# A routed block without its last stage: a token-major output to which the expert rows are added by DMA

## The chip, the cores and the metric

The kernel runs on one core of a Trainium2 chip. Its engines are PE (TensorE, matrix products into the PSUM banks), DVE (VectorE), ACT (ScalarE), POOL (GpSimd) and SP, which here only issues DMAs. Each runs its own instruction list in order and waits on semaphores. The metric is the device time of one execution, in microseconds (us).

## The reference

Eight sequences of 512 tokens, 128 channels. A modulated layer norm feeds a block of time mixing (a recurrence over tokens) and channel mixing; then a second modulated norm feeds a mixture of experts, whose result returns through a gate `gb`, one vector of 128 channels for each sequence:

```python
h = _layernorm(x) * (1 + cb) + sb
x = x + gb * _L0_ffn_ref(h, ...)
# in _L0_ffn_ref:
logits = x @ w_router.T                      # 16 experts, top 1
scores = sigmoid(logits) * mask
gate, up = split(einsum('eth,ehf->etf', scores.T[:, :, None] * x, gate_up_proj))
expert_out = einsum('etf,efh->eth', up * silu(gate), down_proj)
shared = (silu(x @ w_gate.T) * (x @ w_up.T)) @ w_down.T
out = shared + expert_out.sum(axis=0)
```

So each of the 4096 tokens has the residual x, plus gb times the shared expert, plus gb times the row of its one expert. All is float32.

## The kernel before

**Stage 1, attention and routing** (the loops over `NB + LAG`, batches of 512 tokens, four of them in flight). Activations are mostly channel-major: channels on the 128 partitions, tokens along the row. For batch b, DVE's `residual` makes the new residual `x3w`; ACT's `keep_x3` (L764) copies it to `x3_all`; PE's `t3` turns it to token-major in a bank for the norm's statistics. `route`, `chosen`, `rank` and `slots` find each token's expert and its slot in `sorted_rows`, a table in HBM sorted by expert, in which each expert has a room of its own. POOL's `scatter` (L400) writes 128 token rows a time by indirect DMA: 32 of them, four a batch. A row is 132 floats: the scored token and its number.

**Stage 2, shared expert** (`shared_up`, `shared_silu`, `shared_act`, `shared_down`, `shared_base`; batches in pairs after the first two). PE's order is up(0), down(0), a wait for the last slots, up(1), down(1), then up(b), up(b+1), down(b), down(b+1). `shared_base` (L636) adds gb times the result to `x3_all`, channel-major, where gb is one number for each partition. Meanwhile SP fills the rest of each expert's last block with pad rows (L315, 16 DMAs) and loads the first six row blocks into `xb` (L325).

**Stage 3, experts** (`NBLK` = 47 blocks of 128 sorted rows, enough for any split). Per block: SP loads the rows; PE turns them (`row_in`, L1030), multiplies by the expert's gate and up matrices (`gate_up`, 512 columns), turns the activation (`turn_act`, L1043) and multiplies by the down matrix (`down`). ACT copies the turned rows (L827), takes the silu (L831) and copies the result y (L838). DVE copies the token number (L680), makes the product (L681) and copies its transpose (L685). POOL scatters y to its token's row of `y_rows` in HBM (L423); rows with a number over the last token are dropped by the bounds check. PE's order in step s is `turn_act(s-3)`, `down(s-4)`, `row_in(s)`, `gate_up(s-1)`. PE enters the stage when the last `shared_base` is done. A float32 product of 128 or 512 columns shows as two matmul instructions in the trace, a transpose as one.

**Stage 4, the last.** When all scatters have landed, SP reads `y_rows` batch by batch (L333), PE turns it (L862, `turn`), DVE multiplies by gb and adds `x3_all` (L698), ACT's queue stores to the channel-major output (L851). The host transposes it.

The order of all this is written out by hand; no scheduler moves anything. Every helper product on PE has line L858.

Of the kernel before, what the change touches and what calls it, by code (L numbers as in the profile page):

```python
# [3 lines left out]
def program(nc, ins, out_t):  # L4
# [18 lines left out]
    ROW = C + 4  # L23
    ROOM = NB * T + P
    PADS = E * ROOM
    NOROW = NB * T
    LAG = 3
    DEPTH = 6
    ENDS = 4
# [4 lines left out]
    with ctx:  # L34
        def sb(name, shape, dt=F32):
            return ctx.enter_context(nc.sbuf_tensor(name, shape, dt))
# [25 lines left out]
        x3_all = sb("x3_all", [P, NB * T])  # L62
# [69 lines left out]

        at[0] = 0
        yt = [tiles(carve(T)) for _ in range(ENDS)]
        fin = [carve(T) for _ in range(ENDS)]
        pad_row = sb("pad_row", [P, ROW])

# [7 lines left out]

        sorted_rows = nc.dram_tensor("sorted_rows", [PADS + P, ROW], F32, kind="Internal").ap()
        y_rows = nc.dram_tensor("y_rows", [NB * T, C], F32, kind="Internal").ap()
# [19 lines left out]
        L_pads = Signal("L_pads", 1 + E, 16)  # L167
# [5 lines left out]
        K_rows = Signal("K_rows", NB)  # L173

# [51 lines left out]
        C_dn = Signal("C_dn", 1)  # L226
        C_base = Signal("C_base", 1)

# [5 lines left out]
        D_act = Signal("D_act", 2)  # L234
# [3 lines left out]
        D_y = Signal("D_y", 1)  # L238
        D_out = [Signal(f"D_out{q}", 1, 16) for q in range(DEPTH)]

        E_y = [Signal(f"E_y{q}", 1, 16) for q in range(ENDS)]
        E_t = Signal("E_t", 1)
        E_f = Signal("E_f", 1)
        E_out = [Signal(f"E_out{q}", 1, 16) for q in range(ENDS)]

# [19 lines left out]
        def _(sp):  # L265
# [12 lines left out]

            sp.dma_start(cT[:], ins["cT"]).then_inc(L_small.sem, 16)
# [39 lines left out]
            for j in range(NBLK):  # L319
                q, i = j % DEPTH, j // DEPTH  # L320
                at_row = nc.s_assert_within(sp.value_load(table[j:j + 1, 1:2]), 0, PADS,
                                            skip_runtime_bounds_check_because="the table makes it as min(row, PADS)")
# [6 lines left out]
            for b in range(NB):  # L329
                q, i = b % ENDS, b // ENDS  # L330
                if i:
                    sp.wait_ge(E_t.sem, E_t.after(b - ENDS))
                sp.dma_start(yt[q], y_rows[span(b, T), :].rearrange("(j p) c -> p j c", p=P)).then_inc(E_y[q].sem, 16)  # L333

        @block.gpsimd
        def _(pool):
# [11 lines left out]
            pool.memset(pad_row[:, 0:C], 0.0).then_inc(K, 1)  # L348
            pool.memset(pad_row[:, C:ROW].bitcast(I32), NOROW).then_inc(K, 1)
            pool.iota(rows[:, :, C:C + 1].bitcast(I32), pattern=[[P, NTT], [1, 1]], base=0, channel_multiplier=1).then_inc(K, 1)  # L350
            pool.memset(rows[:, :, C + 1:ROW], 0.0).then_inc(K, 1)
# [44 lines left out]
            def scatter(b):  # L396
                pool.wait_ge(A_rows.sem, A_rows.after(b))
                pool.wait_ge(B_slot.sem, B_slot.after(b))
# [20 lines left out]

            for j in range(NBLK):  # L420
                q = j % DEPTH
                pool.wait_ge(D_y.sem, D_y.after(j))
                pool.indirect_dma_start(y_rows, bass.IndirectOffsetOnAxis(number[q], 0), yb[q], None,  # L423
                                        bounds_check=NB * T - 1, oob_is_err=False).then_inc(D_out[q].sem, 16)

        @block.vector
        def _(dve):
# [205 lines left out]
            def shared_base(b):  # L633
                dve.wait_ge(C_dn.sem, C_dn.after(b))
                x3 = x3_all[:, span(b, T)]
                dve.scalar_tensor_tensor(x3, bank[shared_banks[b % 2][0]][:], modc[:, GB, b:b + 1], x3,  # L636
                                         ALU.mult, ALU.add).then_inc(C_base.sem, 1)
# [26 lines left out]
            dve.tensor_scalar(table[:, 1:2], passed[:, 1:2], float(PADS), None, ALU.min).then_inc(S, 1)  # L664
# [10 lines left out]
            def expert_act(j):  # L675
                q = j % DEPTH
                if j >= DEPTH:
                    dve.wait_ge(D_out[q].sem, D_out[q].after(j // DEPTH - 1))
# [8 lines left out]
            for s in range(NBLK + 2):  # L687
                if block_no(s - 2):
                    expert_aT(s - 2)
                if block_no(s - 1):  # L690
                    expert_act(s - 1)

            for b in range(NB):
                q, i = b % ENDS, b // ENDS
                dve.wait_ge(E_t.sem, E_t.after(b))
                if i:
                    dve.wait_ge(E_out[q].sem, E_out[q].after(i - 1))
                dve.scalar_tensor_tensor(fin[q], bank[q][:], modc[:, GB, b:b + 1], x3_all[:, span(b, T)],  # L698
                                         ALU.mult, ALU.add).then_inc(E_f.sem, 1)

        @block.scalar
        def _(act):
# [16 lines left out]
            modulation_rows(0)  # L719

# [55 lines left out]
            for s in range(NB + LAG):  # L776
                if batch(s):
                    norm_rows(A_n1, 0, s, flat(xtok), flat(ht))
                    if s == 0:
                        for n in range(1, NB // 2):  # L780
                            modulation_rows(n)
                        act.wait_ge(K_dve.sem, K_dve.after(0))
                if batch(s - 2):
                    norm_rows(A_n3, 2, s - 2, bank[bX2], n3t)
                    x2(s - 2)
# [47 lines left out]
            def expert_y(j):  # L833
                q = j % DEPTH
                act.wait_ge(D_dn.sem, D_dn.after(j))
                if j >= DEPTH:
                    act.wait_ge(D_out[q].sem, D_out[q].after(j // DEPTH - 1))
                act.copy(yb[q], bank[6 + j % 2][:, 0:C]).then_inc(D_y.sem, 1)  # L838

            for s in range(NBLK + 3):  # L840
# [4 lines left out]
                if block_no(s - 3):  # L845
                    expert_y(s - 3)

            for b in range(NB):
                q = b % ENDS
                act.wait_ge(E_f.sem, E_f.after(b))  # L850
                act.dma_start(out_t[:, span(b, T)], fin[q]).then_inc(E_out[q].sem, 16)  # L851
            for q in range(ENDS):
                act.wait_ge(E_out[q].sem, E_out[q].after(NB // ENDS - 1))

        @block.tensor
        def _(pe):
# [19 lines left out]
            pe.wait_ge(K_dve.sem, K_dve.after(0))  # L876
            pe.wait_ge(L_att.sem, L_att.after(0))
# [192 lines left out]
            for b in range(NB):  # L1070
                q, i = b % ENDS, b // ENDS
                pe.wait_ge(E_y[q].sem, E_y[q].after(i))
                if i:
                    pe.wait_ge(E_f.sem, E_f.after(b - ENDS))
                turn(bank[q], flat(yt[q])).then_inc(E_t.sem, 1)

# [33 lines left out]
```

## Time and profile before

| | |
|---|---|
| median of 3 runs | 395.59 us (393.89 to 396.46) |
| the profiled execution | 393.6 us, span 391.8 us |
| PE busy | 296.8 us (76%) |
| DVE, POOL, ACT busy | 244.0, 187.6, 179.3 us (62%, 48%, 46%) |
| chain that ended last | PE 30%, DVE 24%, POOL 21%, issue 13%, ACT 7%, DMA 3% |
| clock granted to PE, mean | 0.858 |

The span runs from the first to the last instruction. The chain is followed back from the last instruction, at each step to what released it; "issue" is time for which the profile shows no cause. The granted clock is a share of 2.4 GHz: 1.00 is that, 0.50 is 1.2 GHz. POOL's rows for indirect DMAs are the engine's own time on them, not the transfer's; "landing" is from issue until the semaphore has its count. The shares are averages over the four stages.

### The profile page before, as it was taken

Reading aid. Unit: us, or ns where it says so; the run is one execution under the profiler, and the core shown is the slowest. Engines: PE = TensorE matmul, PEld = TensorE weight load, DVE = VectorE, ACT = ScalarE, POOL = GpSimd, SP = SyncE. Lnnn points to the kernel's source line nnn. Section 1 sums busy time; section 2 is a strip of 40 time slices with the busy share of each in tenths; the row PEclk is TensorE's granted clock in tenths of the full one; section 3 lists DMA queues with packets and bytes.
Section 4 is the critical chain, followed back from the end, with each engine's and each line's share of the span. In section 5 each row is a group of like instructions: output and inputs, shape, how many; then the busy total and the mean of one; then the engine's idle time right before and its main releaser. Section 6 shows DMA issues by size and latency. Waiting matters only on the chain.

```text
span 391.8 us, 4364 instructions
## 1 busy us (share of the span) xinstructions
PE 296.8 (76%) x1140; PEld 171.7 (44%) x1140; DVE 244.0 (62%) x514; ACT 179.3 (46%) x436; POOL 187.6 (48%) x267
## 2 busy tenths in 40 slices
PE   4363667877668766877795586699989999999844
PEld 4223234334433534544453343334436666666532
DVE  5148596997989889789688342634335444444423
ACT  2541654947556666555372543222214444444300
POOL 4542726558678485656273534310003666666610
PEclk9956598996998888767889598699999999999955
DMA  6688000102011010010010100132002222222057
GB/s 182 175 241 321 28 0 4 51 0 60 22 47 35 0 54 29 0 41 21 0 49 8 41 14 14 50 97 49 0 1 56 75 75 82 71 77 71 4 155 274
DMA packets 28184, 25.22 MB, mean 64 GB/s; under 512 B 3682, under 2 KB 21734, under 8 KB 28160
## 3 DMA queue, kind: packets, MB, share of 16 engines
q1 hardware_dynamic: 24480, 18.57, 16.5%
q0 software_dynamic: 2528, 4.27, 3.4%
q10 hardware_dynamic: 1152, 2.10, 1.4%
q8 instruction: 10, 0.16, 0.2%
q14 instruction: 14, 0.11, 0.1%
HBM read 17.42 MB, written 8.49 MB: 66 GB/s over the span
## 4 chain that ended last, share of the span: by engine, by line
PE 30%; DVE 24%; POOL 21%; issue 13%; ACT 7%; DMA 3%; SPq 0%; POOLq 0%; DVEq 0%; ACTq 0%
PE bank L858 23%; POOL y_rows L423 11%; PE bank L862 5%; DVE work L524 4%; POOL sorted_rows L400 4%; POOL work L377 3%; ACT work L724 2%; DMA work<-y_rows 2%; DVE work L543 2%; DVE work L519 2%; DVE work L517 1%; DVE work L541 1%; PE bank L901 1%; POOL work L381 1%; DVE work L528 1%
## 5 line engine op out<-in xcount | busy, mean ns | idle before, releaser
L423 POOL DMA_INDIRECT y_rows<-work x47 | 46.2, 982 | 71.2 <-ACT work L838 41.9
L862 PE MATMUL bank<-ident,work 128*128 128x128 f32 x192 | 40.2, 362 | 52.9 <-ACT work L724 23.9
L862 PEld LDWEIGHTS bank<-ident,work 128*128 128x128 f32 x192 | 29.9, 185 | 75.0 <-ACT work L724 28.9
L858 PE MATMUL bank<-up_experts,work 128*128 x94 | 48.2, 595 | 0.0
L685 DVE COPY work<-bank 128x256 f32<-128x256 f32 x47 | 19.9, 424 | 37.7 <-PE bank L1043 37.7
L400 POOL DMA_INDIRECT sorted_rows<-rows,slot_i x32 | 36.5, 1140 | 14.4 <-issue 8.9
L858 PE MATMUL bank<-work,Fk 128*128 128x512 f32 x64 | 34.9, 652 | 5.7 <-DVE work L506 5.7
L724 ACT ACTIVATE work<-work 128x128 f32<-128x128 f32 x64 | 26.3, 487 | 23.5 <-POOL work L381 23.5
L375 POOL TENSOR_SCALAR work<-work 128x4 f32<-128x4 f32 x32 | 6.7, 210 | 59.5 <-DVE work L432 58.6
L377 POOL TENSOR_TENSOR work<-work,neghalf 128x4 f32<-128x4 f32 x32 | 33.2, 1038 | 2.7
L858 PE MATMUL bank<-work,Fv 128*128 128x512 f32 x64 | 33.3, 648 | 0.0
L724 ACT ACTIVATE work<-bank,work 128x128 f32<-128x128 f32 x64 | 24.1, 459 | 13.9 <-POOL work L381 13.8
L831 ACT ACTIVATE work<-bank 128x256 f32<-128x256 f32 x47 | 18.0, 383 | 25.4 <-PE bank L858 25.4
L858 PE MATMUL bank<-down_experts,work 128*128 x188 | 28.9, 276 | 0.1
L394 POOL TENSOR_TENSOR work<-work 128x512 f32<-128x512 f32 x16 | 16.8, 1068 | 23.5 <-ACT work L756 23.4
L524 DVE RECIPROCAL work<-work 128x512 f32<-128x512 f32 x8 | 26.8, 3346 | 0.0
L858 PEld LDWEIGHTS bank<-down_experts,work 128*128 128x128 f32 x188 | 24.7, 191 | 0.3 <-issue 0.3
L1043 PEld LDWEIGHTS bank<-ident,work 128*128 128x128 f32 x94 | 12.9, 139 | 25.6 <-DVE work L681 16.3
L819 ACT ACTIVATE work<-bank 128x512 f32<-128x512 f32 x16 | 9.4, 597 | 29.8 <-PE bank L858 28.7
L756 ACT ACTIVATE work<-bank 128x512 f32<-128x512 f32 x32 | 18.6, 601 | 5.8 <-PE bank L858 5.7
L631 DVE TENSOR_TENSOR work<-work,bank 128x512 f32<-128x512 f32 x16 | 10.9, 686 | 15.1 <-PE bank L858 14.4
L858 PEld LDWEIGHTS bank<-work,Fk 128*128 128x128 f32 x64 | 11.4, 210 | 19.3 <-DVE work L506 13.8
(161 smaller groups left out, 630.4 us busy)
## 6 DMA issues: line engine op xcount, KB each, us to landing
up_experts<-in_gate_up SPq DMA_DIRECT2D x2, 2048.0 KB, 11.7
work<-sorted_rows SPq DMA_DIRECT2D x47, 66.0 KB, 1.8
work<-in_x SPq DMA_DIRECT2D x8, 256.0 KB, 3.4
work<-in_xT SPq DMA_DIRECT2D x8, 256.0 KB, 3.1
work<-y_rows SPq DMA_DIRECT2D x8, 256.0 KB, 4.2
out_t<-work ACTq DMA_DIRECT2D x8, 256.0 KB, 3.9
sorted_rows<-pad_row SPq DMA_DIRECT2D x17, 66.0 KB, 1.6
y_rows<-work POOLq DMA_INDIRECT x47
```

The lines of the kernel that those rows point to most:

```text
L377: pool.tensor_tensor(rstd[n], rstd[n], neghalf[:], ALU.pow).then_inc(S.sem, 1)
L394: pool.tensor_tensor(relus[c], relus[c], relus[c], ALU.mult).then_inc(A_sqp.sem, 1)
L400: pool.indirect_dma_start(sorted_rows, bass.IndirectOffsetOnAxis(slot_i[:, n:n + 1], 0), rows[:, n, :], None).then_inc(B_out.sem, 16)
L423: pool.indirect_dma_start(y_rows, bass.IndirectOffsetOnAxis(number[q], 0), yb[q], None, bounds_check=NB * T - 1, oob_is_err=False).then_in ...
L524: dve.reciprocal(ek, ek).then_inc(S.sem, 1)
L685: dve.tensor_copy(aT[j % 2], bank[4 + j % 2][:, 0:F]).then_inc(D_aT.sem, 1)
L724: act.activation(dst[:, j * C:(j + 1) * C], src[:, j * C:(j + 1) * C], ACT.Identity, bias=shift[n][:, j:j + 1], scale=rstd[n][:, j:j + 1]) ...
L756: act.activation(relus[c], bank[(bFK, bFK2)[k % 2]][:], ACT.Relu).then_inc(A_relu.sem, 1)
L831: act.activation(sge[j % 2], bank[2 + j % 2][:, 0:F], ACT.Silu).then_inc(D_sg.sem, 1)
L858: return pe.matmul(out, w, x, start=start, stop=stop)
L862: last = pe.transpose(out[:, j * P:(j + 1) * P], src[:, j * P:(j + 1) * P], ident[:])
L1043: last = pe.transpose(bank[4 + j % 2][:, c * P:(c + 1) * P], acte[j % 2][:, c * P:(c + 1) * P], ident[:])
```

## The change

The output becomes token-major, with 31 blocks of spare rows behind the 4096 tokens, which the host cuts off. `x3` is kept token-major (`x3_rows`), copied by ACT from the bank in which `t3` turned it. The shared expert's down product is made with the tokens on the partitions, so gb runs along the row: POOL multiplies `Wd` by gb for each batch (`Wd_gb`, two buffers), and `shared_base` is a plain addition. SP stores each batch's base to the output (`base_out`), four before the pad copies and four behind them. Rows in `sorted_rows` grow from 132 to 260 floats: scored token, gb, number. gb comes there by four DMAs between on-chip buffers. Pad rows lie ready in HBM, each with a spare row's number of its own, and the 16 pad DMAs copy from there. In the expert stage DVE multiplies y by the row's gb and POOL adds the block to the output by an accumulating indirect DMA without bounds check, after all bases have landed. The last stage and `y_rows` are gone. In the diff below a header names the engine.

```diff
-    ROW = C + 4
+    ROW = 2 * C + 4
+    NUM = 2 * C
...
-    NOROW = NB * T
+    SPARE = NBLK - NTT
...
@@ SP (sync)
+            def base_out(b):
+                sp.wait_ge(C_base.sem, C_base.after(b))
+                sp.dma_start(tokens(out_t[0:NB * T].rearrange("(b t) c -> b t c", b=NB), b), tiles(x3_rows[:, b])).then_inc(C_out.sem, 16)
...
+            sp.wait_ge(K_gb.sem, K_gb.after(0))
+            for j in range(NT):
+                sp.dma_start(rows[:].rearrange("p (b j) r -> p b j r", j=NT)[:, :, j, C:2 * C], gb_rows[:]).then_inc(L_gb.sem, 16)
...
-            sp.dma_start(sorted_rows[PADS:PADS + P, :], pad_row[:]).then_inc(L_pads.sem, 16)
+            pads = sorted_rows[PADS:, :].rearrange("(k p) r -> p k r", p=P)
+            sp.dma_start(pads[:, :, 0:NUM], pad_row[:].rearrange("p (o r) -> p o r", o=1).broadcast_to([P, SPARE + E, NUM])).then_inc(L_pads.sem, 16)
+            sp.dma_start(pads[:, :, NUM:], pad_id[:]).then_inc(L_pads.sem, 16)
             for b in range(NB - LAG + 1, NB):
                 load_xT(b)
+            for b in range(NB // 2):
+                base_out(b)
+            sp.wait_ge(L_pads.sem, L_pads.after(0, 2))
             sp.wait_ge(B_table.sem, B_table.after(0, 1))
             for e in range(E):
...
-                sp.dma_start(sorted_rows[bass.ds(at_row, P), :], pad_row[:]).then_inc(L_pads.sem, 16)
+                sp.dma_start(sorted_rows[bass.ds(at_row, P), :], sorted_rows[PADS + (SPARE + e) * P:PADS + (SPARE + e + 1) * P, :]).then_inc(L_pads.sem, 16)
+            for b in range(NB // 2, NB):
+                base_out(b)
...
                 if i:
-                    sp.wait_ge(D_act.sem, D_act.after(j - DEPTH))
+                    sp.wait_ge(D_y.sem, D_y.after(j - DEPTH))
                 sp.dma_start(xb[q], sorted_rows[bass.ds(at_row, P), :]).then_inc(D_x[q].sem, 16)
...
-            for b in range(NB):
...
-                sp.dma_start(yt[q], y_rows[span(b, T), :].rearrange("(j p) c -> p j c", p=P)).then_inc(E_y[q].sem, 16)
@@ POOL (gpsimd), behind the loop that ends with scatter(7)
+            for b in range(NB):
+                if b >= 2:
+                    pool.wait_ge(C_dn.sem, C_dn.after(b - 2))
+                pool.tensor_tensor(Wd_gb[:, b % 2], Wd[:], gb_rows[:, b:b + 1, :].broadcast_to([P, FC, C]), ALU.mult).then_inc(C_scale.sem, 1)
+
+            pool.wait_ge(C_out.sem, C_out.after(NB - 1))
             for j in range(NBLK):
                 q = j % DEPTH
                 pool.wait_ge(D_y.sem, D_y.after(j))
-                pool.indirect_dma_start(y_rows, bass.IndirectOffsetOnAxis(number[q], 0), yb[q], None,
-                                        bounds_check=NB * T - 1, oob_is_err=False).then_inc(D_out[q].sem, 16)
+                pool.indirect_dma_start(out_t, bass.IndirectOffsetOnAxis(number[q], 0), yb[q], None,
+                                        compute_op=ALU.add).then_inc(D_out[q].sem, 16)
@@ DVE (vector)
-                dve.scalar_tensor_tensor(x3, bank[shared_banks[b % 2][0]][:], modc[:, GB, b:b + 1], x3,
-                                         ALU.mult, ALU.add).then_inc(C_base.sem, 1)
+                dve.tensor_tensor(x3_rows[:, b], bank[shared_banks[b % 2][0]][:], x3_rows[:, b], ALU.add).then_inc(C_base.sem, 1)
...
             def expert_act(j):
...
-                dve.tensor_copy(number[q], xb[q][:, C:C + 1].bitcast(I32)).then_inc(D_act.sem, 1)
...
+            def expert_y(j):
+                q = j % DEPTH
+                if j >= DEPTH:
+                    dve.wait_ge(D_out[q].sem, D_out[q].after(j // DEPTH - 1))
+                dve.tensor_copy(number[q], xb[q][:, NUM:NUM + 1].bitcast(I32)).then_inc(D_y.sem, 1)
+                dve.wait_ge(D_dn.sem, D_dn.after(j))
+                dve.tensor_tensor(yb[q], bank[6 + j % 2][:, 0:C], xb[q][:, C:2 * C], ALU.mult).then_inc(D_y.sem, 1)
+
+            for s in range(NBLK + 3):
                 if block_no(s - 2):
                     expert_aT(s - 2)
                 if block_no(s - 1):
                     expert_act(s - 1)
+                if block_no(s - 3):
+                    expert_y(s - 3)
-            for b in range(NB):
...
-                dve.scalar_tensor_tensor(fin[q], bank[q][:], modc[:, GB, b:b + 1], x3_all[:, span(b, T)],
-                                         ALU.mult, ALU.add).then_inc(E_f.sem, 1)
@@ ACT (scalar)
+            def gb_copy(n):
+                act.wait_ge(K_gbm.sem, n + 1)
+                act.copy(gb_rows[:, n * NT:(n + 1) * NT, :], tok(5 + n)).then_inc(K_gb.sem, 1)
...
             def keep_x3(b):
-                act.wait_ge(A_x3.sem, A_x3.after(b))
-                act.copy(x3_all[:, span(b, T)], x3w).then_inc(A_keep.sem, 1)
+                act.wait_ge(A_st[3].sem, A_st[3].after(b))
+                act.copy(x3_rows[:, b], bank[bT3][:]).then_inc(A_keep.sem, 1)
...
-            def expert_y(j):
...
-                act.copy(yb[q], bank[6 + j % 2][:, 0:C]).then_inc(D_y.sem, 1)
...
-                act.dma_start(out_t[:, span(b, T)], fin[q]).then_inc(E_out[q].sem, 16)
@@ PE (tensor)
+            for b in range(NB):
+                last = mm(bank[5 + b // NT][:, b % NT * C:(b % NT + 1) * C], modc[:, GB, b:b + 1].broadcast_to([P, P]), ident[:])
+                if b % NT == NT - 1:
+                    last.then_inc(K_gbm.sem, 1)
...
             def shared_down(b):
                 q = b % 2
                 pe.wait_ge(C_act.sem, C_act.after(b))
-                for c in range(FC):
-                    last = mm(bank[shared_banks[q][0]][:], Wd[:, c], sg[q][c], start=c == 0, stop=c == FC - 1)
+                pe.wait_ge(C_scale.sem, C_scale.after(b))
+                for j in range(NT):
+                    for c in range(FC):
+                        last = mm(bank[shared_banks[q][0]][:, j * C:(j + 1) * C], sg[q][c][:, j * P:(j + 1) * P], Wd_gb[:, q, c],
+                                  start=c == 0, stop=c == FC - 1)
                 last.then_inc(C_dn.sem, 1)
...
-            for b in range(NB):
...
-                turn(bank[q], flat(yt[q])).then_inc(E_t.sem, 1)
```

## Rows read from the trace of the kernel before

**Rows 1.** Chain of waits, last 26 us: start us, us, what

```profile
372.63 2.12 DMA y_rows<-work
...
374.89 0.39 SPq L333
...
388.54 0.75 DVE work L698
```

**Rows 2.** Stretches: busy us of each engine, granted clock, DMA share, GB/s

```profile
213.50:216.40 2.90, 0.01 (x1) 0.00 (x0) 2.69 (x6) 1.50 (x4) 0.89 (x3) 0.90 0.01 3
216.40:218.50 2.10, 1.97 (x8) 1.57 (x8) 0.76 (x2) 0.06 (x1) 0.06 (x1) 0.50 0.37 120
...
236.60:240.30 3.70, 3.70 (x8) 2.10 (x9) 0.76 (x2) 0.59 (x1) 1.47 (x3) 0.58 0.00 0
...
258.00:291.00 33.00, 32.88 (x76) 14.36 (x76) 12.82 (x19) 7.16 (x12) 0.00 (x0) 1.00 0.12 31
290.70:291.90 1.20, 0.18 (x1) 0.00 (x0) 0.75 (x1) 0.00 (x0) 0.00 (x0) 1.00 0.00 0
```

**Rows 3.** Timeline, start of the shared expert: start, us, engine, line, operation

```profile
250.19 3.53 PE L858 MATMUL bank<-work,Wd 128*128 128x512 f32 x4 [1.49 <-DVE work L631]
...
255.28 0.96 POOL L400 DMA_INDIRECT sorted_rows<-rows,slot_i  x1 [0.31 <-issue]
...
257.26 0.69 DVE L631 TENSOR_TENSOR work<-work,bank 128x512 f32<-128x512 f32 x1 [0.17 <-PE bank L858]
...
258.00 1.98 PE L858 MATMUL bank<-work,Wd 128*128 128x512 f32 x4 [0.85 <-DVE work L631]
```

**Rows 4.** Timeline, two of the pairs of shared_down

```profile
266.69 3.60 PE L858 MATMUL bank<-work,Wd 128*128 128x512 f32 x8
...
276.99 3.60 PE L858 MATMUL bank<-work,Wd 128*128 128x512 f32 x8
```

**Rows 5.** Timeline, end of the shared and start of the expert stage

```profile
290.92 0.75 DVE L636 SCALAR_TENSOR_TENSOR x_all<-bank,modc,x_all 128x512 f32<-128x512 f32 x1 [0.96 <-PE bank L858]
...
291.93 0.30 PE L1030 MATMUL bank<-ident,work 128*128 128x128 f32 x1 [1.05 <-DVE x_all L636]
```

**Rows 6.** Timeline, one step of the expert stage

```profile
357.45 1.02 PE L858 MATMUL bank<-up_experts,work 128*128 x2
...
358.73 0.42 DVE L685 COPY work<-bank 128x256 f32<-128x256 f32 x1 [0.82 <-PE bank L1043]
358.87 0.14 PEld L1030 LDWEIGHTS bank<-ident,work 128*128 128x128 f32 x1
...
359.09 1.02 PE L858 MATMUL bank<-up_experts,work 128*128 x2
359.13 0.41 DVE L681 TENSOR_TENSOR work<-work,bank 128x256 f32<-128x256 f32 x1
359.18 0.27 ACT L838 COPY work<-bank 128x128 f32<-128x128 f32 x1 [0.28 <-PE bank L858]
...
360.21 0.98 POOL L423 DMA_INDIRECT y_rows<-work  x1 [0.65 <-issue]
```

**Rows 7.** SP's row loads; page on them; last, xT's (256 KB)

```profile
266.32 4.42 SPq L325 DMA_DIRECT2D work<-sorted_rows  x6
...
work<-sorted_rows SPq DMA_DIRECT2D x47, 66.0 KB, 1.8
...
DMA to landing us min/median/max: 2.7/3.1/3.6
```

**Rows 8.** Timeline, end of the expert stage

```profile
371.12 0.27 ACT L838 COPY work<-bank 128x128 f32<-128x128 f32 x1 [0.55 <-PE bank L858]
...
372.63 0.98 POOL L423 DMA_INDIRECT y_rows<-work  x1 [0.30 <-issue]
```

**Rows 9.** Timeline, set-up

```profile
12.04 1.27 POOL L388 TENSOR_TENSOR work<-work,ca_rows 128x512 f32<-128x512 f32 x1 [2.65 <-ACT work L724]
...
17.65 1.65 ACT L724 ACTIVATE work<-work 128x128 f32<-128x128 f32 x4 [3.85 <-POOL work L381]
```

More of the change, by code:

```diff
@@ L61, in program @@
         h2_all = sb("h2_all", [P, NB * T])
-        x3_all = sb("x3_all", [P, NB * T])
+        x3_rows = sb("x3_rows", [P, NB, T])
+        gb_rows = sb("gb_rows", [P, NB, C])
+        Wd_gb = sb("Wd_gb", [P, 2, FC, C])
         rows = sb("rows", [P, NTT, ROW])
@@ L130, in program @@
         number = [carve(1).bitcast(I32) for _ in range(DEPTH)]
[L133 to L136, printed above, removed]
+        pad_row = sb("pad_row", [P, NUM])
+        pad_id = sb("pad_id", [P, SPARE + E, ROW - NUM])
         bank = [ctx.enter_context(nc.psum_tensor(f"bank{n}", [P, 512], F32)) for n in range(8)]
@@ L144, in tok @@
             return bank[n][:].rearrange("p (j c) -> p j c", c=C)
-        sorted_rows = nc.dram_tensor("sorted_rows", [PADS + P, ROW], F32, kind="Internal").ap()
-        y_rows = nc.dram_tensor("y_rows", [NB * T, C], F32, kind="Internal").ap()
+        sorted_rows = nc.dram_tensor("sorted_rows", [PADS + (SPARE + E) * P, ROW], F32, kind="Internal").ap()
         class Signal:
@@ L173, in program @@
         K_rows = Signal("K_rows", NB)
+        K_gbm = Signal("K_gbm", 2)
+        K_gb = Signal("K_gb", 2)
+        L_gb = Signal("L_gb", NT, 16)
         A_x = Signal("A_x", 1, 16)
@@ L237, in program @@
         D_dn = Signal("D_dn", 1)
-        D_y = Signal("D_y", 1)
+        D_y = Signal("D_y", 2)
         D_out = [Signal(f"D_out{q}", 1, 16) for q in range(DEPTH)]
[L241 to L244, printed above, removed]
         g1, b1, g2, b2, tm1, cm1, tdec, tfirst, tm2, cm2 = (vecs[:, n:n + 1] for n in range(10))
@@ L320, in _ @@
                 q, i = j % DEPTH, j // DEPTH
-                at_row = nc.s_assert_within(sp.value_load(table[j:j + 1, 1:2]), 0, PADS,
-                                            skip_runtime_bounds_check_because="the table makes it as min(row, PADS)")
+                at_row = nc.s_assert_within(sp.value_load(table[j:j + 1, 1:2]), 0, PADS + (SPARE - 1) * P,
+                                            skip_runtime_bounds_check_because="the table makes it as min(row, last)")
                 if i:
-                    sp.wait_ge(D_act.sem, D_act.after(j - DEPTH))
+                    sp.wait_ge(D_y.sem, D_y.after(j - DEPTH))
                 sp.dma_start(xb[q], sorted_rows[bass.ds(at_row, P), :]).then_inc(D_x[q].sem, 16)
@@ L347, in _ @@
                                pattern=[[1, P]], channel_multiplier=-1).then_inc(K, 1)
[L348 to L351, printed above, removed]
+            pool.memset(pad_row[:], 0.0).then_inc(K, 1)
+            pool.iota(pad_id[:].bitcast(I32), pattern=[[P, SPARE + E], [0, ROW - NUM]], base=NB * T, channel_multiplier=1).then_inc(K, 1)
+            pool.iota(rows[:, :, NUM:NUM + 1].bitcast(I32), pattern=[[P, NTT], [1, 1]], base=0, channel_multiplier=1).then_inc(K, 1)
+            pool.memset(rows[:, :, NUM + 1:ROW], 0.0).then_inc(K, 1)
             for t in (x1p, x2p):
@@ L397, in scatter @@
                 pool.wait_ge(A_rows.sem, A_rows.after(b))
+                if b == 0:
+                    pool.wait_ge(L_gb.sem, L_gb.after(0))
                 pool.wait_ge(B_slot.sem, B_slot.after(b))
@@ L663, in _ @@
             dve.wait_ge(S, 12)
-            dve.tensor_scalar(table[:, 1:2], passed[:, 1:2], float(PADS), None, ALU.min).then_inc(S, 1)
+            dve.tensor_scalar(table[:, 1:2], passed[:, 1:2], float(PADS + (SPARE - 1) * P), None, ALU.min).then_inc(S, 1)
             shared_base(0)
@@ L782, in _ @@
                         act.wait_ge(K_dve.sem, K_dve.after(0))
+                        gb_copy(0)
+                        gb_copy(1)
                 if batch(s - 2):
@@ L831, in expert_silu @@
                 act.activation(sge[j % 2], bank[2 + j % 2][:, 0:F], ACT.Silu).then_inc(D_sg.sem, 1)
-            def expert_y(j):
[L834 to L837, printed above, removed]
-                act.copy(yb[q], bank[6 + j % 2][:, 0:C]).then_inc(D_y.sem, 1)
-            for s in range(NBLK + 3):
+            for s in range(NBLK + 1):
                 if block_no(s):
@@ L1068, in _ @@
                     gate_up(s - 1, e_up)
[L1070 to L1074, printed above, removed]
-                turn(bank[q], flat(yt[q])).then_inc(E_t.sem, 1)
 def kernel(**inputs):
@@ L1105 @@
     ins = {n: nc.dram_tensor(f"in_{n}", a.shape, mybir.dt.float32, kind="ExternalInput").ap() for n, a in arrays.items()}
[L1106 removed]
+    out_t = nc.dram_tensor("out_t", (nb * nt + (2 * ne - 1) * 128, c), mybir.dt.float32, kind="ExternalOutput").ap()
     program(nc, ins, out_t)
     got = run_bass_kernel_spmd(nc, [{f"in_{n}": a for n, a in arrays.items()}], core_ids=[0])
[L1109 removed]
+    return np.ascontiguousarray(got.results[0]["out_t"][:nb * nt]).reshape(nb, nt, c)
```

27 lines of the change are left out of this document (5 added, 22 removed).

## The prediction

> **What bounds the kernel now.** I read the chain of waits first, at its end. The last expert scatter starts at 372.63 and has landed 2.12 us later, at 374.75; only then does SP issue the first read of y_rows (374.89), and the last vector instruction starts at 388.54 with a store behind it [rows 1]. So everything from 374.75 to the end of the 391.8 us span, 17.05 us, is the last stage, and nothing else runs beside it.
>
> Then the table of stretches, for TensorE (PE) and its clock. From 258 to 291, the shared expert, PE is busy 32.88 of 33.00 us at full clock, 2.4 GHz [rows 2]: what is added to PE there is added to the time. Two batches take 10.30 us (276.99 less 266.69) [rows 4]. The same table shows the clock's cost: PE did nothing for 2.90 us from 213.50 and the next matmuls ran at 0.50, 1.2 GHz; after another such gap 236.60 to 240.30 still averaged 0.58; a gap of 1.2 us from 290.70 kept 1.00 [rows 2].
>
> The expert stage repeats every 1.64 us (359.09 less 357.45), and PE sets it: two 512-column pieces of 0.43 us (1.72 us for four, by rows 4: 10.30 us over 24 pieces) and seven 128-column pieces in the remaining 0.78 us, so 0.11 us each [rows 4, 6]. GpSimd (POOL) needs 0.98 us and then waits 0.65 [rows 6]; at the end, with the last scatter already due, it idles only 0.30 us before it [rows 8]. POOL's own limit is therefore 0.98 + 0.30 = 1.28 us a block.
>
> **What the change removes.** The eight reads, 32 transposes, eight combines and eight stores, with SP's, PE's, DVE's and ACT's waits: 17.05 us [rows 1]. The new end is the landing of the last scatter.
>
> **The start of the shared expert.** This is the largest cost. shared_down(0) now waits for Wd_gb, which POOL makes behind its 32nd scatter. That one starts at 255.28 and takes 0.96 us [rows 3]; a multiply of 128x512 took 1.27 us [rows 9], so 128x256 about 0.64, and with 0.2 us of hand-over PE starts at about 257.1 in place of 250.19 [rows 3]: +6.9 us. Queued behind it on PE are shared_up(1) and all that follows; DVE and ACT wait with it. down(0) was cold already (four pieces in 3.53 us) [rows 3]; it becomes 16 pieces of 128 columns, which cold cost 0.246 us each (x8 in 1.97) [rows 2], 3.9 us: +0.5 with the later return of the clock (0 to 1.5).
>
> **The other seven shared_down.** 16 x 0.11 = 1.79 us in place of 4 x 0.43 = 1.72 on the bound engine: 7 x 0.08 = +0.6. The later Wd_gb each have a pair's 10.30 us to be made in [rows 4]. shared_base turns from 0.75 us into a plain addition (0.69, as row 257.26) [rows 3, 5]: -0.06, left out.
>
> **The start of the expert stage.** The first row block used to be on chip; PE's transpose started at 291.93, 0.26 us after the last base (290.92 + 0.75) [rows 5]. Now SP issues base_out(7) on that signal, reads the table, and only then loads. SP's reaction is 0.14 us [rows 1], an issue with its table read 0.82 us ((4.42 - 0.33) / 5) [rows 7], so the load starts about 1.0 us behind the base and lands 2.1 us later, and the 256 KB store ahead of it in SP's queue (2.5 to 3.1 us for such sizes, as xT) may hold it to about 3.3: 3.3 - 0.26 = +3.1 us (2.6 to 4). The 16 pad copies stand behind base_out(3), but 16 x 0.82 = 13 us fit before the last base. PE is then idle for over 4 us, longer than the gap that halved the clock [rows 2]; the 0.58 from 236.60 to 240.30 is 3.1 us at half speed, 1.6 us lost, of which the filling pipeline hides part: +1.3 (0 to 2).
>
> **The loop over the row buffers.** The buffer is freed later: before, DVE's product freed it; now the gated product of y, two steps later. Follow one round. gate_up starts at 357.45; its product runs 359.13 to 359.54, so 2.09 us on. In DVE's order the number copy and the y of two blocks earlier come next: 0.06 + 0.32 (a 128x128 product by the line through 0.41 for 256 and 0.69 for 512 columns is 0.27 us, and 0.05 of start) makes 2.47 us [rows 3, 6]. Then 0.14 for SP, the load, 0.09 to reach PE, and 0.22 from row_in's weight load (358.87) to gate_up (359.09) [rows 6]. This y is block j - 6, whose step stands three steps ahead of row_in(j), so the period is at least (2.92 + load) / 3. A load of 528-byte rows lands in 1.8 us [rows 7]: 1.57, hidden. Rows are now 1040 bytes. xT, 128 rows of 2048 bytes, takes 2.7 at best, 3.1 in the middle [rows 7]; interpolated, 2.1 to 2.25. I take 2.1, and with the accumulate's traffic beside it 2.15: 1.69 us a block, +0.05 over the 41 blocks that reuse a buffer = +2.0 us. Bounds: 0 (a load of 1.95 is hidden) and +8 (2.6, 1.84 us a block).
>
> The Trainium skill, DMA: Bandwidth & Descriptors, Anatomy of one DMA, fits a DMA as a constant plus bytes at 436 GB/s, for the GpSimd path. By it the 65.5 KB more would cost 0.15 us, the loop would stay hidden, and the sum would be 2.0 us lower. The xT row, 0.9 us more for 194 KB at its best, speaks for the dearer line here.
>
> **DVE and ACT in this loop.** DVE's idle 0.82 us a block before the copy of L685 takes in the 0.3 [rows 6]; ACT loses 0.27. No cost, while the period is over 1.3 us. POOL gets y 0.4 us later, once: at the end y's last piece comes 0.27 us behind PE either way, and three scatters in a row at 1.28 make +0.3.
>
> **The accumulating scatter.** No row shows one. Nearest are the plain scatters, 0.96 and 0.98 us on POOL and 2.12 us to landing [rows 1, 3, 8]. Lower bound: the same. Upper bound: twice the POOL time, since it handles two sources for each row. I take the same POOL time, by those rows, and +0.4 for the last landing (0 to 2). A price up to 1.38 us on POOL is hidden by the 1.69 us loop.
>
> **Small edits.** The 16 pieces for the gate on PE (1.8 to 3.9 us by the rates above) and two ACT copies fall in the 3.85 us in which ACT idled before row 17.65 [rows 9]: +0.3 (0 to 1). The x3 copy waits for statistics that the normalisation behind it waits for anyway: 0. Wider scatters have as many rows: 0. Four 0.5 MB gate copies (512-byte pieces) behind the expert weights, and 4 MB of pads in two DMAs on SP's queue, run where that queue is nearly idle; the next loads have several us: 0, and if SP is held past xT(6)'s issue, some us.
>
> **Sum.** -17.05 + 6.9 + 0.5 + 0.6 + 3.1 + 1.3 + 2.0 + 0.3 + 0.4 + 0.3 = -1.65. The profiled execution took 393.6 us, 2.0 under the median of 395.59; carried to the median, 394.
>
> **Rivals.**
> (A) The waits stay small: clock restarts hide in the pipeline, the load lands in under 1.95, the scatter is plain. -17.05 + 6.9 + 0.6 + 2.6 + 0.5 = -6.4, about 389. For it: three of my terms have 0 as a bound. Against it: the 6.9 and 2.6 are order in the code.
> (B) Slower: POOL becomes the bound of the expert stage through the accumulate. It decides from 1.38 us a scatter on (0.98 now). At one and a half times, 1.47 + 0.30 = 1.77 a block, 47 x 0.13 = +6.1 in place of +2.0: 398. At twice, 2.26, +29 in place of +2: 421. For it: POOL's time is per row, and rows get a second source. Against: 0.98 holds a fixed part, and bounds checking goes.
> The Trainium skill, Collectives: The Full Stack, Stop 4, shows an adding DMA as two reads and one write, and its GPSIMD Engine Reference, When to use GPSIMD, has one core write the read descriptors and another the write descriptors; by that the reading core's work doubles, the 421 end of this rival. No row here shows it.
> (C) The accumulate's extra read and write slow the loads beside it: a landing of 2.8 gives 1.91 us a block, +11: 403. Before, they shared the engines with plain scatters and stayed at 1.8 [rows 7], against it.
>
> **Chances.** Forecast 0.42, A 0.20, B 0.25 (a third of it at the far end), C 0.13. About 1%, 4 us, is what a measurement tells from no change. Faster by more: A, mostly, and a little of the forecast: 0.22. Within: 0.38. Slower: B, C and the forecast's upper part: 0.40. The likeliest case alone spans 390 to 398. The range takes in A nearly whole, C, and B at half more: 389 to 408.
>
> **What would show it.** PE idle from before 250.2 until about 257, with POOL's multiply ending it; row_in(0) some 3 us behind the last base, at clock 0.50; gate_up every 1.69 us and row_in waiting for DMA, not POOL; scatters of 0.98 us; the end 2.5 us behind the last scatter's start. Scatters over 1.38 us, or gate_up at 1.64 us with no clock loss, would make it wrong, upwards or downwards.

## The result: 3% slower

The changed kernel took 407.14 us (median of 4 runs, 406.25 to 408.11), the kernel before 395.22 beside it (4 runs, 393.89 to 396.46): ratio 1.030, 95% interval 1.026 to 1.035. The profiled execution took 406.78 us, its span is 404.5, against 393.6 and 391.8 before. Here and below a median is over all runs of a kernel and a ratio over its faster runs alone, because the times of one kernel fall into groups some 6 us apart; so a ratio need not be that of the two medians. The forecast was 394; what came is rival B and, on top, an end that no case had.

**Profile after.** From the page: POOL's busy time, and its busy tenths in 40 slices of 10.1 us, where the last stage is gone and POOL stands at 8 from slice 32 on:

```profile
PE 295.5 (73%) x1220; PEld 178.5 (44%) x1220; DVE 247.2 (61%) x553; ACT 172.1 (43%) x391; POOL 221.6 (55%) x275
...
POOL 5542636558557584873444523501101888888884
...
L438 POOL DMA_INDIRECT out_t<-work x47 | 73.5, 1564 | 36.3 <-DVE work L703 24.7
```

The line of the output scatter (duration min/median/max in ns, first and last start; then the landings) answers to the 0.98 us and 2.12 us of [rows 1, 8]:

```profile
L438 POOL DMA_INDIRECT out_t<-work x47: 1559/1562/1634, 311.5 to 397.5; - x47
...
DMA to landing us min/median/max: 3.2/3.4/4.4
```

1.56 us, and 0.30 of issue behind each: the chain of waits (start, us, what) goes from one scatter to the next and finds no other engine:

```profile
380.69 1.56 POOL out_t L438
382.26 0.30 issue
382.56 1.56 POOL out_t L438
```

Next the timeline at the start of the shared expert, which answers to [rows 3]. POOL's multiply follows the 32nd scatter, and PE, idle for 8.48 us, starts at 257.86 in place of 250.19:

```profile
255.99 0.96 POOL L409 DMA_INDIRECT sorted_rows<-rows,slot_i  x1 [0.30 <-issue]
256.98 1.41 POOL L432 TENSOR_TENSOR Wd_gb<-Wd,gb_rows 128x256 f32<-128x256 f32 x2
257.86 3.38 PE L860 MATMUL bank<-Wd_gb,work 128*128 128x128 f32 x16 [8.48 <-POOL Wd_gb L432]
...
265.52 0.71 PE L860 MATMUL bank<-Wd_gb,work 128*128 128x128 f32 x4 [0.85 <-DVE work L646]
```

And the start of the expert stage, against [rows 5]: the last base ends at 299.62, SP loads from 300.59, and PE's first transpose starts at 303.12, 3.50 us behind the base (0.26 before). The product of 512 columns takes 1.92 us until the clock is back, then 1.05:

```profile
298.93 0.69 DVE L650 TENSOR_TENSOR x_rows<-bank,x_rows 128x512 f32<-128x512 f32 x1 [1.09 <-PE bank L860]
300.59 10.67 SPq L337 DMA_DIRECT2D work<-sorted_rows  x7
303.12 0.45 PE L1040 MATMUL bank<-ident,work 128*128 128x128 f32 x1 [4.24 <-DMA work<-sorted_rows]
...
304.17 1.92 PE L860 MATMUL bank<-up_experts,work 128*128 x2
...
308.44 1.05 PE L860 MATMUL bank<-up_experts,work 128*128 x2
```

Stretches of the changed kernel (from:to, length, busy us of PE, PEld, DVE, ACT, POOL, granted clock, DMA share, GB/s), beside [rows 2]: PE full in the shared expert, then nothing for 3.5 us, then half clock:

```profile
265.50:299.00 33.50, 33.37 (x160) 21.70 (x160) 12.48 (x19) 7.17 (x12) 3.65 (x5) 1.00 0.35 99
299.60:303.10 3.50, 0.00 (x0) 0.01 (x1) 0.02 (x1) 0.00 (x0) 0.00 (x0) 0.79 0.76 207
303.10:306.10 3.00, 2.65 (x6) 1.24 (x7) 0.00 (x0) 0.53 (x2) 0.00 (x0) 0.50 0.62 154
```

Last, what stands behind the final scatter: the line of the wrapper that closes each engine's list (operation, duration, start). POOL's DRAIN is reached by the sequencer at 390.1, with scatters still queued ahead of it, and ends at 404.3; the scatters have landed at 400.9, when SP is done:

```profile
L34 POOLq DRAIN  x1: 14165/14165/14165, 390.1 to 390.1; - x1
L34 SPq COMPARE_BRANCH  x1: 42/42/42, 401.0 to 401.0; - x1
```

**The ledger**, from like landmarks of both traces, in us of span (stage 1 ends where PE begins to wait for down(0), at 248.70 before and 249.38 after):

| piece | predicted | measured |
|---|---|---|
| stage 1, to the end of its work | +0.3 | +0.7 |
| down(0) waits for Wd_gb | +6.9 | +7.0 |
| down(0) itself, to down(1) | +0.5 | -0.15 |
| the other seven, to the last base | +0.6 | +0.4 |
| last base to row_in(0) | +3.1 | +3.2 |
| row_in(0) to the first output scatter | +1.3 | +2.3 |
| first to last output scatter (74.5 to 86.0) | +2.3 | +11.4 |
| last scatter's start to the end (19.2 to 7.0) | -16.65 | -12.2 |
| sum | -1.65 | +12.7 |

Two lines carry the miss: 9.1 us in the expert stage, 4.5 at the end. In the line from first to last scatter, the predicted +2.3 is +2.0 for the row buffers and +0.3 for the last scatters.

### The profile page after: what moved, and what is told of

It is laid out like the page before. It is cut to its first block, busy times and chain, and to the rows that moved or that the text cites. A ratio compares the mean times of both kernels' runs of the same rounds, so it can differ in the third digit from the quotient of the medians.

```text
span 404.5 us, 4394 instructions
## 1 busy us (share of the span) xinstructions
PE 295.5 (73%) x1220; PEld 178.5 (44%) x1220; DVE 247.2 (61%) x553; ACT 172.1 (43%) x391; POOL 221.6 (55%) x275
## 4 chain that ended last, share of the span: by engine, by line
PE 40%; DVE 25%; POOL 15%; ACT 6%; issue 5%; DMA 5%; SPq 1%; POOLq 1%; DVEq 0%; ACTq 0%
PE bank L860 32%; POOL sorted_rows L409 4%; PE bank L864 4%; DMA work<-sorted_rows 4%; DVE work L539 4%; POOL out_t L438 3%; POOL work L384 3%; ACT work L740 2%; PE bank L1053 2%; DVE work L558 2%; DVE work L534 2%; DVE work L532 1%; PE bank L1040 1%; PE bank L908 1%; DVE work L556 1%
## 5 line engine op out<-in xcount | busy, mean ns | idle before, releaser
L438 POOL DMA_INDIRECT out_t<-work x47 | 73.5, 1564 | 36.3 <-DVE work L703 24.7
L864 PE MATMUL bank<-ident,work 128*128 128x128 f32 x160 | 30.7, 339 | 40.5 <-ACT work L740 20.8
L860 PE MATMUL bank<-up_experts,work 128*128 x94 | 50.2, 617 | 0.0
L864 PEld LDWEIGHTS bank<-ident,work 128*128 128x128 f32 x160 | 23.1, 173 | 60.3 <-ACT work L740 29.6
L860 PE MATMUL bank<-work,Fv 128*128 128x512 f32 x64 | 34.2, 662 | 0.0
L845 ACT COPY work<-bank 128x128 f32<-128x128 f32 x47 | 12.5, 266 | 30.8 <-PE bank L1040 30.8
L837 ACT ACTIVATE work<-bank 128x512 f32<-128x512 f32 x16 | 9.4, 597 | 36.9 <-PE bank L860 35.9
L1053 PEld LDWEIGHTS bank<-ident,work 128*128 128x128 f32 x94 | 13.0, 141 | 25.8 <-DVE work L691 14.1
L691 DVE TENSOR_TENSOR work<-work,bank 128x256 f32<-128x256 f32 x47 | 19.3, 410 | 6.9 <-ACT work L849 6.9
L860 PE MATMUL bank<-Wd_gb,work 128*128 128x128 f32 x128 | 16.6, 291 | 9.3 <-POOL Wd_gb L432 8.5
```

What stands on the lines that cost most here:

```text
L438: pool.indirect_dma_start(out_t, bass.IndirectOffsetOnAxis(number[q], 0), yb[q], None, compute_op=ALU.add).then_inc(D_out[q].sem, 16)
L860: return pe.matmul(out, w, x, start=start, stop=stop)
L864: last = pe.transpose(out[:, j * P:(j + 1) * P], src[:, j * P:(j + 1) * P], ident[:])
L1053: last = pe.transpose(bank[4 + j % 2][:, c * P:(c + 1) * P], acte[j % 2][:, c * P:(c + 1) * P], ident[:])
```

## The experiments

**Theory.** The stage runs at POOL's own time for an accumulating scatter, and the kernel ends with POOL's drain, not with the landing. Rivals: the traffic of the accumulate slows the row loads; the loop over the row buffers is the longer one; the end is the landing of the data.

**1. The changed kernel with a plain scatter.** It leaves out the addition of the base: the expert rows overwrite it.

```diff
-                                        compute_op=ALU.add).then_inc(D_out[q].sem, 16)
+                                        ).then_inc(D_out[q].sem, 16)
```

> The changed kernel with a plain indirect scatter in place of the accumulating one (leaves out the addition: routed rows overwrite the base). Theory A, the addition itself makes POOL's scatter long: 1.56 us falls to 0.96 to 0.98, POOL stops being the bound, the period falls from 1.87 to the row-buffer loop's (2.92 + 2.2) / 3 = 1.71, 46 x 0.16 = 7.3 us less: 399.8 us. Rival, the length comes from the wide destination, the missing bounds check or the spare rows: scatter and time stay, 407.

397.42 us (10 runs, 392.26 to 399.67), ratio 1.013 (1.004 to 1.022). The output scatter's line:

```profile
L438 POOL DMA_INDIRECT out_t<-work x47: 960/960/1010, 312.4 to 389.0; - x47
...
DMA to landing us min/median/max: 2.2/2.3/4.1
```

The stage takes 76.6 us in place of 86.0 (1.665 a block). The row loads land in 2.1 us with the plain scatter and in 2.2 with the accumulating one: the traffic did not slow them. 9.4 us belong to the scatter's form.

**2. The kernel before with an accumulating scatter**, into y_rows set to zero by one DMA in stage 1; all else stays.

```diff
-                                        bounds_check=NB * T - 1, oob_is_err=False).then_inc(...)
+                                        bounds_check=NB * T - 1, oob_is_err=False, compute_op=ALU.add).then_inc(...)
```

> The kernel before with one part of the change alone: its scatter into y_rows (zeroed beforehand by one DMA) accumulates; bounds check, narrow rows and last stage stay. Theory A: scatter 0.98 becomes 1.56, the period 1.64 becomes 1.87, 46 x 0.23 = 10.6 us more: 406. Rival: scatter stays 0.98 and the time at 395.

406.6 us (4 runs, 405.68 to 406.78), ratio 1.037 (1.025 to 1.050). Here row buffers, row size and DVE's list are the old ones, and the stage still takes 85.9 us, 1.867 a block:

```profile
L424 POOL DMA_INDIRECT y_rows<-work x47: 1557/1562/1612, 298.9 to 384.8; - x47
```

The same 1.56 us with the bounds check as without it, on narrow rows and on the old table. This one word costs 11.4 us from first to last scatter, nearly the 12.7 of span that the whole change lost.

**3. The kernel before without its last stage.** It leaves the expert rows out of the output; SP stores the bases.

```diff
+            for b in range(NB):
+                sp.dma_start(out_t[:, span(b, T)], x3_all[:, span(b, T)]).then_inc(E_out[0].sem, 16)
...
-                turn(bank[q], flat(yt[q])).then_inc(E_t.sem, 1)
```

> The kernel before without its last stage; SP stores x3_all (shared part only) beside the expert stage's end, so the output lacks the expert rows. Theory B, POOL's own drain ends a kernel whose last work is a scatter: last scatter's start at 372.6 plus 6.8 to 7.5, span 380, time 382: the last stage costs 11.7 us beyond what ends anyway. Rival, the end is the landing (2.1 us behind the start): span 375, time 377, as the prediction's 17.05 had it.

381.13 us (4 runs, 378.81 to 385.0), ratio 0.973 (0.955 to 0.991); span 377.0. The drains:

```profile
L34 POOLq DRAIN  x1: 8187/8187/8187, 368.6 to 368.6; - x1
L34 SPq DRAIN  x1: 13/13/13, 371.7 to 371.7; - x1
```

The last scatter starts at 369.24 and has landed when SP passes its waits, at 371.7; POOL's drain ends at 376.8 and the span with it. From the last scatter's start the end comes after 7.8 us in place of 19.2: the last stage is worth 11.4 us to whoever removes it, not 17.

**4. The changed kernel, POOL waiting for the landings before it stops.** It tells whether the drain waits for data or works.

```diff
+            for q in range(DEPTH):
+                pool.wait_ge(D_out[q].sem, D_out[q].after((NBLK - 1 - q) // DEPTH))
```

> The changed kernel, and POOL waits at its end for the landing of all its output scatters, as SP does, before it stops. In the changed kernel the last scatter leaves POOL at 399.08, all have landed at 400.9, and POOL's drain ends at 404.3. If the drain waits for the transfers and for little else, it ends with or within 1 us of where it does now, 403.5 to 404.5. If it is a piece of POOL's own work that begins only when the drain is reached, it starts at 400.9 and takes its 5.2 us: the span ends near 406. If it is POOL's own work that is already under way behind each scatter (a fixed distance behind the last one), the end stays at 404.3 within 0.3 us.

One run, 407.73 us, span 406.0, and the drain now stands by itself:

```profile
L34 POOLq COMPARE_BRANCH  x1: 41/41/41, 400.4 to 400.4; - x1
...
L34 POOLq DRAIN  x1: 5213/5213/5213, 400.6 to 400.6; - x1
```

Everything has landed, nothing is queued, and it still takes 5.21 us. In the changed kernel it ends 5.2 us behind the last scatter's end on POOL (399.08 to 404.3). So the drain is not a wait for the data: it is work of its own, begun when POOL reaches it.

**5. The row-buffer loop: eight buffers in place of six**, with the plain scatter of run 1 (the same part left out), so that POOL hides nothing.

```diff
-    DEPTH = 6
+    DEPTH = 8
```

> The plain-scatter kernel (leaves out the addition) with eight row buffers in place of six. If with a plain scatter the buffer loop bounds the expert stage at 1.71 us, as the prediction worked it out, eight buffers free it: period 1.64, PE's own, 46 x 0.07 = 3.2 us less than with six: 396.5. Rival, the loop never bounds: same as with six buffers.

395.39 us (10 runs, 389.94 to 398.64), ratio 1.002 (0.996 to 1.009). First to last scatter:

```profile
L438 POOL DMA_INDIRECT out_t<-work x47: 960/960/1008, 311.0 to 385.6; - x47
```

74.6 us against 76.6: 2.0 us, the size of the term, but not by its mechanism. The steady distance of two scatters is 1.64 us in both traces; the predicted 1.69 stands in neither. What six buffers cost in run 1 are three single waits of `row_in` for a row block that landed late (3.5, 2.9 and 2.8 us, where the median is 2.1); with eight buffers there is no such wait after the first scatter:

```profile
318.60 0.14 PEld L1039 LDWEIGHTS bank<-ident,work 128*128 128x128 f32 x1 [1.19 <-DMA work<-sorted_rows]
...
338.92 0.14 PEld L1039 LDWEIGHTS bank<-ident,work 128*128 128x128 f32 x1 [0.65 <-DMA work<-sorted_rows]
...
355.89 0.14 PEld L1039 LDWEIGHTS bank<-ident,work 128*128 128x128 f32 x1 [0.53 <-DMA work<-sorted_rows]
```

With a landing of 2.1 the prediction's formula gives 1.67 a block, so its 2.92 us for the rest of the round is at least 0.1 too long. In the changed kernel all this lies under POOL's 1.87 and costs nothing.

**6. The scale factors earlier:** scale(0) and scale(1) ahead of the last four scatters in POOL's order.

```diff
+                if s - 4 == NB - 1:
...
+                    scale(0)
+                    scale(1)
                 if batch(s - 4):
                     scatter(s - 4)
```

> The changed kernel with the first two products Wd_gb ahead of POOL's last four scatters. If PE's wait for POOL is worth what the prediction gave it: shared_down(0) starts about 7.0 us earlier and all behind it too: 400.2 us. Rival, another wait takes its place (PE cold, or POOL as the bound of the end absorbs it): under 3 us, 404 or more.

399.09 us (4 runs, 398.23 to 399.55), ratio 1.019 (1.007 to 1.031): 8 us of the changed kernel's loss back. 7.0 of them are shown: PE's idle time before down(0) is 1.50 us, not 8.48. The rest is mostly stage 1, which ended 1.5 us earlier in this profile. The multiplies stand in a gap in which POOL waits for slots anyway (4.38 us still idle before the last four scatters, 5.58 without them):

```profile
249.40 3.51 PE L867 MATMUL bank<-Wd_gb,work 128*128 128x128 f32 x16 [1.50 <-DVE work L653]
```

**7. The base stores issued from ACT's queue**, so that SP can load the first row blocks in the shared stage.

```diff
-            for b in range(NB // 2):
-                base_out(b)
...
+                act.dma_start(out_t[span(b, T)].rearrange("(j p) c -> p j c", p=P), tiles(x3_rows[:, b])).then_inc(C_out.sem, 16)
```

> The changed kernel with the bases stored from ACT's queue, so that SP can load the first six row blocks while the shared expert runs, as before. If the late start of the expert stage is SP's order: row_in(0) 0.3 us behind the last base in place of 3.5 (-3.2), and no cold clock in the filling (-2.3): 401.6 us. Rival, the filling of the pipeline or the base's landing sets it anyway: 404 to 407.

401.12 us (4 runs, 398.14 to 402.53), ratio 1.017 (1.011 to 1.023).

```profile
297.10 0.30 PE L1039 MATMUL bank<-ident,work 128*128 128x128 f32 x1 [0.99 <-DVE x_rows L641]
297.67 0.30 PE L1039 MATMUL bank<-ident,work 128*128 128x128 f32 x1 [0.26 <-issue]
297.84 1.12 PE L859 MATMUL bank<-up_experts,work 128*128 x2
```

From down(1) to row_in(0) it is 34.36 us in place of 37.60 (-3.2), and from there to the first output scatter 6.35 in place of 8.43 (-2.1): the product is at 1.12 us at once. The first two products carry 1.8 of it (2.44 us from the first gate_up to the third, 4.27 in the changed kernel), so most of the second piece was the clock's; the rest goes with the second row block, which is on chip here and was waited for there. Between down(0) and down(1) this profile loses 1.6 us again: 9.3 us at a mean granted clock of 0.67, where the changed kernel took 7.7 at 0.82. The median's 6 us include a stage 1 that ended 4.4 us earlier.

**8. Both moves together** (edits 6 and 7).

> Early Wd_gb and stores from ACT together. If the two are separate: -7.0 and -5.5, 394.6 us, level with the kernel before. Rival, they overlap because POOL's 47 scatters at 1.87 us set the end either way: 398 or more.

392.44 us (10 runs, 389.34 to 398.31), ratio 0.998 (0.992 to 1.005). Scatters at 1.57 us, 295.9 to 382.1, still 1.87 a block: what is left to gain is POOL's. From the end of stage 1 to the end it takes 144.7 us, the changed kernel 155.1, the kernel before 143.1.

**9 to 11. A plain output scatter that still adds the base.** Run 8's kernel, but POOL scatters the bases, during the shared stage, with the same slots into a second sorted table; SP loads a base block beside each row block; DVE adds it. These three leave nothing out.

```diff
+                    pool.indirect_dma_start(sorted_base, bass.IndirectOffsetOnAxis(slot_i[:, b * NT + n:b * NT + n + 1], 0),
+                                            x3_rows[:, b, n * C:(n + 1) * C], None).then_inc(C_sort.sem, 16)
...
+                dve.tensor_tensor(yb[j % YD], yb[j % YD], bb[j % BD], ALU.add).then_inc(D_add.sem, 1)
```

> Built on the version with both moves (scale factors ahead of the last four scatters; no base stores on SP). The base no longer goes to the output: POOL scatters it, behind each shared_base, with the same slots into a second sorted table in HBM (32 more plain scatters, in the shared stage, where POOL is idle most of the time), SP loads a base block of 64 KB beside each row block, DVE adds it to the product, and POOL's scatter to the output is plain, without compute. The sum against the version with both moves (its profiled span 389.1, median 392.4): the first product is made at the same place, 295.9; the 32 base scatters at 1.28 us end near 310 and land near 313, so the first output scatter leaves only near 316, and from there POOL catches up at 1.28 a block while PE makes a block each 1.65: the products end near 295.9 + 46 x 1.65 = 371.8, the scatters near 377; then POOL's drain, 7.5 behind the last scatter's start. If the accumulating scatter's own time on POOL is what sets 1.87 a block: span 383 to 386, time 384 to 389, faster than the kernel before by 1.5 to 2.5%. If instead 1.87 a block is set by the traffic of the stage (more bytes in HBM, the same now with another load in it), the stage keeps 1.85 or more a block and the time is 391 to 394. If DVE, with one more operation of some 0.25 us a block, becomes the bound: 1.75 a block, time near 391.

411.05 us (6 runs, 409.7 to 414.91), ratio 1.051 (1.044 to 1.059). The scatter is back at 0.96 us, but DVE waits for base blocks only just issued (waits between 320 and 405: us, times, longest):

```profile
DVE work L749 <- DMA work<-sorted_base: 30.3, 33, 2.4
```

The second try issued base blocks four steps ahead (`for n in adds(s + AHEAD)`).

> The version with the sorted base (plain output scatters of 0.96 us) ran at 411.0, because each base block was loaded only after the wait of one step: DVE stood 30.3 us in 33 waits for a base block that had just been issued (landing 2.4). Here the base blocks are loaded four steps ahead of their addition, the row blocks three steps ahead, and the first addition stands at step 12 (the base scatters leave POOL by 302.5 and land by 304.5, step 12 is near 310). If those waits were the whole of it: the first output scatter near 311, the products end near 297 + 46 x 1.65 = 373, the last scatter near 375, POOL's drain 7.5 behind its start: span 381 to 384, time 384 to 388, faster than before by 1.5 to 2.5%. If the stage is set by the traffic of its loads (three DMAs a block) it stays at 1.8 or more a block: 390 to 395. If DVE's longer list is the bound, 1.75 a block: near 389.

418.59 us (6 runs, 414.29 to 420.92), ratio 1.067 (1.056 to 1.078): missed again. Traffic does not hold it: over the output scatters run 11 moves 156 GB/s, this run 133 (from 320 to 400 us). SP's queue, where it runs free, issues one load each 0.81 us, so two are 1.62 a block with no room for its waits, which now stood in front of each other's loads:

```profile
344.96 0.33 SPq L349 DMA_DIRECT2D work<-sorted_rows  x1
345.77 0.33 SPq L357 DMA_DIRECT2D work<-sorted_base  x1
346.58 0.33 SPq L349 DMA_DIRECT2D work<-sorted_rows  x1
```

The third reads one address for both loads, has 20 base buffers, and loads the first 12 base blocks from ACT's queue.

> In the two versions with the sorted base SP issued two loads a block, each behind a read of its address; no two of them stood closer than 0.81 us (0.33 of it the DMA's own issue), 1.62 a block, and each also waited in order for other work: the stage ran at 1.8 to 2.2 a block. Here one address serves both loads of a block (about 1.15 us of SP a block), the ring of base blocks has 20 buffers instead of 8, and the first 12 base blocks are loaded from ACT's queue, one a step from step 8 on. If SP's issue and the order of its waits were what held the stage: first product near 297, 1.62 to 1.7 a block for the products, which end near 373; first output scatter near 311, last near 376, drain 7.5: span 382 to 386, time 385 to 389, faster than before by 1.5 to 2.5%. If the traffic holds it, or DVE's longer list: 1.8 or more a block, 392 or more.

390.05 us (12 runs, 385.33 to 394.25) against 393.97 (19 runs); ratio 0.997 (0.990 to 1.003). From down(0)'s start to the end it takes 138.4 us in its profile; the kernel before 141.6, run 8 143.2, the changed kernel 146.6.

```profile
L473 POOL DMA_INDIRECT out_t<-work x47: 952/958/1052, 316.9 to 381.4; - x47
...
L36 POOLq DRAIN  x1: 11323/11323/11323, 380.2 to 380.2; - x1
L36 SPq DRAIN  x1: 7/7/7, 384.3 to 384.3; - x1
```

POOL starts late and catches up at 1.40 a block. From the end of stage 1 to the end it is 15 us under the changed kernel (139.9 for 155.1); against the kernel before, the interval includes no change. Its span ends 10.4 us behind that last scatter, not 7.5, and that is POOL's drain again (L36 is the wrapper's line in this kernel): all has landed at 384.3, and the drain ends at 391.5, 9.1 us behind the scatter's end. Runs 9 and 10 show the same 9.1 and 9.2. These three kernels issue 32 indirect DMAs more, 111 in place of 79.

## Why the prediction was wrong

**The accumulating scatter is the step that failed.** It said "I take the same POOL time, by those rows"; measured, 1.56 us, 1.6 times the plain one (runs 1 and 2). Its own bounds held this, and 1.56 is beyond the turning point of rival B. That point, 1.38 us, leant on a loop of 1.69 that no trace shows; by the measured 1.64 it is 1.34. With 1.56 + 0.30 = 1.87 against 1.64, the rival's arithmetic gives 47 x 0.23 = 10.8 in place of +2.0, some 403. The argument "rows get a second source" pointed the right way, though no run shows what POOL does in the longer time; the value was taken at the end of the range that cost nothing. Where a cost decides from 1.4 times on and lies between one and two, the rival should have been the forecast. From the Trainium skill (Collectives: The Full Stack, Stop 4, which shows two reads and one write, and GPSIMD Engine Reference, When to use GPSIMD) the prediction worked out a doubling; the 1.6 measured is less.

**The new end is the second.** The prediction put it at "the landing of the last scatter". It is POOL's drain: 5.2 us of work when POOL has nothing left (run 4). The changed kernel ends 7.0 us behind the last scatter's start, 3.6 behind its landing. Before, the same line ran under the last stage:

```profile
L34 POOLq DRAIN  x1: 8210/8210/8210, 371.9 to 371.9; - x1
```

It ended at 380.1, with 11.7 us of other work behind it. So the removed stage covered something that nobody needed to see, and removing it gained 12.2 us, not 16.65. These 4.5 us and the 9.1 of the stage make 13.6 of the 14.3 us of span between forecast and result.

**That 407 lies within the range of 389 to 408 is luck.** The cases that it was to take in reached 398 (B at one and a half times) and 403 (C); none had the drain, and the forecast had the change slightly faster.

**What held.** down(0)'s wait (+7.0 for +6.9; run 6 takes it away), the later row_in(0) (+3.2 for +3.1) and the filling at half clock (+2.3 for +1.3; run 7 takes both away but 0.2), and the seven products (+0.4 for +0.6). A row block of 130 KB landed in 2.2 us, where the interpolation with the traffic gave 2.15. The estimate by the Trainium skill (DMA: Bandwidth & Descriptors, Anatomy of one DMA) was 1.8 + 0.15, about 1.95; the measurement is above it. Rival C fell: loads land in 2.2 us beside accumulating scatters, 2.1 beside plain ones. Rival A's cheap end for the clock fell too.

**What did not hold, and cost nothing here.** The row-buffer loop as a steady bound: its +2.0 was met in size by three late loads (run 5). And down(0) itself: -0.15 for +0.5 in the changed kernel, but +1.5 in the profiles of runs 1, 7 and 8 (9.3 us to down(1) for 7.8 before, granted clock 0.67 for 0.80); what makes the clock come back later there is open.

**Where the expected gain went:** 12.2 us were gained at the end; 7.0 + 3.2 + 2.3 were paid at two waits that a different order removes (runs 6 to 8), and 11.4 to POOL, which only a kernel without the accumulating scatter got back (runs 1 and 11).

## What to carry to other kernels

Before an indirect DMA is made to accumulate, measure it on POOL (here, with 128 rows of 512 bytes, 1.6 times the plain one), and ask whether the engine's slack per block (here 0.36 us) covers it. When a last stage is removed, look for what ended under it, the drains of the other engines first. A value made on a queue behind long work delays its reader by all of that work: moving two multiplies ahead of four scatters took a wait of 7.0 us away. And a term that comes out right in size is not yet right: look for its period in the trace.

## Unexpected about the hardware

- POOL's drain: 5.21 us with all transfers landed (run 4). It ends 5.2 us after the last scatter's end where the 47 output scatters accumulate, 6.5 to 6.6 where they are plain (before, runs 1, 3 and 5), and 9.1 to 9.2 in runs 9 to 11. The plain kernels fit a length in proportion to the indirect DMAs issued in the whole kernel: 6.5 us for 79 and 9.1 for 111 are both 0.082 us each. That is an estimate from two counts; no run changed the number alone, and why the accumulating ones leave less is open.
- The accumulating scatter took 1.56 us on POOL with and without a bounds check, and landed in 3.4 us (3.2 in run 2) in place of 2.3 in run 1.
- The granted clock of the same stage differs from kernel to kernel: from 120 to 180 us it was 0.83 in the profile of before, 0.88 in that of the changed kernel, 0.94 in those of runs 3, 7 and 8, whose stage 1 ended 4 to 5 us earlier. Hence the comparisons above from landmark to landmark.
